# Four adaLN layers in one program: the ternary network starts between the turns of its LayerNorm, chunk sums move to the end of a chunk, and local attention loads early

## What is computed

```python
h = layernorm(x) * (1 + ca) + sa;  x = x + ga * attn(h)
h = layernorm(x) * (1 + cb) + sb;  x = x + gb * ffn(h)
```

```python
h = silu((x @ w1.T) * s1) * ((x @ w2.T) * s2)
h = gelu((h @ h1.T) * sh1);  h = gelu((h @ h2.T) * sh2);  return (h @ w3.T) * s3
```

## Time and profile before

| | |
|---|---|
| time, median of 3 runs | 3133.0 us (3131.6 to 3141.1) |
| profiled execution | 3132.21 us, span 3130.4 us |
| busy, share of the span | TensorE 91%, VectorE 73%, ScalarE 64%, GpSimd 40% |
| chain that ended last | TensorE 66%, VectorE 11%, issue 10%, ScalarE 7% |
| mean granted TensorE clock | 0.928 of full speed |

### The profile page before, as it was taken

One profiled execution on the slowest core, in us unless ns is written; L12 is line 12 of the kernel. 1 busy time (PEld: TensorE's weight loads), 2 busy tenths in 40 slices (PEclk: granted clock), 3 DMA queues, 4 the chain that ended last, 5 costly groups with the idle time before them and its releaser, 6 DMA issues.

```text
span 3130.4 us, 88186 instructions
## 1 busy us (share of the span) xinstructions
PE 2859.3 (91%) x36340; PEld 1713.5 (55%) x36340; DVE 2283.3 (73%) x3908; ACT 2010.7 (64%) x5733; POOL 1239.3 (40%) x959
## 2 busy tenths in 40 slices
PE   5689898878898999998699999999999999999997
PEld 3454577523344233333366666666666666666664
DVE  4740486289604777775688888888888888888885
ACT  5542565274313466666488888878888778887784
POOL 0110012000001111111477766766766776677662
PEclk7589955889999899999799999999999999999999
DMA  2000100000001100000332223323332333322221
GB/s 108 3 1 0 38 4 3 1 0 1 0 0 36 46 24 23 21 23 9 134 72 69 73 65 103 76 65 99 69 81 63 96 81 70 93 65 68 68 62 48
DMA packets 48240, 153.41 MB, mean 49 GB/s; under 512 B 11552, under 2 KB 13856, under 8 KB 45952
## 3 DMA queue, kind: packets, MB, share of 16 engines
q1 hardware_dynamic: 47872, 148.17, 18.1%
HBM read 43.60 MB, written 5.44 MB: 16 GB/s over the span
## 4 chain that ended last, share of the span: by engine, by line
PE 66%; DVE 11%; issue 10%; ACT 7%; POOL 2%; DVEq 1%; POOLq 1%; DMA 1%; ACTq 0%; SPq 0%
PE ps L1675 14%; PE ps L798 7%; PE ps L1693 5%; PE ps L1728 5%; DVE arena L1174 4%; PE ps L1737 4%; PE ps L1750 4%; PE ps L1269 4%; PE ps L1297 3%; PE ps L1710 3%; PE ps L1284 3%; PE ps L1719 3%; PE ps L1756 2%; DVE arena L2143 1%; PE ps L1702 1%
## 5 line engine op out<-in xcount | busy, mean ns | idle before, releaser
L1675 PE MATMUL ps<-arena 128*128 128x512 f32 x1152 | 562.0, 610 | 17.9 <-ACTq L1962 16.3
L2027 ACT ACTIVATE arena<-ps,arena 128x64 f32<-128x64 f32 x1536 | 460.1, 320 | 86.5 <-DVE arena L2223 81.4
L2300 POOL TENSOR_TENSOR arena<-arena 128x1024 f32<-128x1024 f32 x190 | 447.6, 2361 | 98.5 <-DVE arena L2112 98.5
L2306 POOL TENSOR_TENSOR arena<-arena 128x2048 f32<-128x2048 f32 x95 | 344.4, 3625 | 225.0 <-ACT arena L1969 219.8
L1435 DVE TENSOR_REDUCE arena<-ps 128x1 f32<-128x512 f32 x512 | 329.3, 686 | 78.1 <-PE ps L1269 73.1
L1396 ACT ACTIVATE arena<-ps 128x1024 f32<-128x1024 f32 x256 | 262.5, 1025 | 179.1 <-PE ps L1284 178.6
L2027 ACT ACTIVATION_READ_ACCUMULATOR arena<-ps,arena 128x1 f32 x1536 | 324.1, 211 | 0.0
L1675 PEld LDWEIGHTS ps<-arena 128*128 128x128 f32 x1152 | 196.9, 190 | 182.6 <-issue 158.0
L2107 DVE TENSOR_TENSOR arena<-ps,arena 128x1024 f32<-128x1024 f32 x192 | 234.1, 1219 | 47.8 <-PE ps L1675 33.3
L194 POOL TENSOR_SCALAR rstd<-mv 128x4 f32<-128x4 f32 x32 | 7.3, 227 | 645.6 <-DVE mv L180 644.4
L2112 DVE TENSOR_TENSOR arena<-ps,arena 128x512 f32<-128x512 f32 x384 | 245.3, 680 | 0.0
(11 more groups left out here) (291 smaller groups left out, 5560.5 us busy)
## 6 DMA issues: line engine op xcount, KB each, us to landing
arena<-pack_l SPq DMA_DIRECT2D x144, 256.0 KB
arena<-grow SPq DMA_DIRECT2D x144, 256.0 KB
arena<-in_deep SPq DMA_DIRECT2D x6, 2649.5 KB, 10.8
arena<-pack_l SPq DMA_DIRECT2D x96, 128.0 KB
arena<-grow SPq DMA_DIRECT2D x84, 128.0 KB
arena<-in_rotary SPq DMA_DIRECT2D x6, 1024.0 KB, 7.4
pack_tern<-in_tern SPq DMA_DIRECT2D x2, 2888.0 KB, 10.4
arena<-scr_q SPq DMA_DIRECT2D x96, 48.0 KB
```

Source lines behind the costliest of these rows:

```text
L1675: last = T.matmul(m.ps[0:rows.stop - rows.start, at + half, :], f.xs[t % 2][:, rows], w.wqkv[:, j * INNER + half * BLK:j * INNER + (half + ...
L2027: last = A(f.prob[:, p, :], m.ps[:, 4 + j % 2, i * SPAN:(i + 1) * SPAN], ACT.Exp, bias=f.nmax[t % 2][:, p:p + 1], accum_out=f.rsum[t % 2][ ...
L2300: G.tensor_tensor(f.rot[t % 2][:, here], f.rot[t % 2][:, here], f.sin[:, here], ALU.add)
L2306: G.tensor_tensor(r, r, spread(f.ss[t % 2], DH), ALU.mult).then_inc(s["rotated"], 1)
```

## The change

Five edits go together.

1. **Chunk sums at the end.** In `gla_vector` the two calls `summed(n - 1)` and `normed(n - 2)` move from ahead of the level work to behind it. In `gla_scalar`, for layer 0, `squares(n - 1)` moves ahead of the second part of the exponentials.
2. **Ternary networks between the turns.** In layers 0 and 2 the meeting ahead of the feed-forward part goes (`MEETINGS` lists those that stay). `tern_tensor` now issues the turns itself: 0 and 1, pair 0, turn 2, pair 1, turn 3, pair 2. Each of the first four pairs waits for as many modulations as its blocks and banks need, by a new semaphore `modulated`. The sixth LayerNorm turns into banks 4 to 7.
3. **First batch in the last pair.** In `mha_tensor` the turn and the output products of batch 0 (`flat(0)`, `projected(0)`) are issued within the last pair; VectorE copies the turned tiles instead of ScalarE, and adds blocks 0 and 1 before it normalises batch 1. The output products go to other banks (`MHA_OUT`).
4. **Attention's first loads.** VectorE clears only the first operand set, GpSimd the other three, and SyncE waits for GpSimd (`vcopied`) ahead of stacks 1 and 2. ScalarE issues the deep stage's first weights and first rotary table before its first exponential, once regrouping has landed; SyncE no longer does so after the meeting.
5. **Two semaphores less.** The loads of the constants and of the modulation weights share one semaphore, and the first Silu waits for both.

The eighth LayerNorm has its own place for the normalised tiles (`m.xn` is now a list), so that it doesn't touch the early table.

```diff
 def mod_scalar(nc, act, m, s):
-    act.wait_ge(m.loaded["const"], 16)
+    act.wait_ge(m.loaded["const"], 32)
...
-LN_BANKS = (0, 4, 0, 4, 0, 0, 0, 4)
+LN_BANKS = (0, 4, 0, 4, 0, 4, 0, 4)
...
         for pair in range(pairs):
             picks(n, pair)
+        if g.layer == 0 and n:
+            squares(n - 1)
         if quarter >= 1:
             decays(quarter + 1, ahead[2:])
         if g.layer == 1:
             squares(n)
-        elif n:
-            squares(n - 1)
...
-        if n:
-            summed(n - 1)
-        if n >= 2:
-            normed(n - 2)
         if quarter + 1 < TILES // CHUNKS:
...
             differences(quarter + 2, LEVEL_OPS[:4])
+        if n:
+            summed(n - 1)
+        if n >= 2:
+            normed(n - 2)
...
+    k = 2 * f.layer + 1
+    ln_tensor(nc, pe, m, ln, k, (0, 1))
     pe.wait_ge(m.loaded["tern"], f.loaded)
...
             if n >= 4:
                 pe.wait_ge(s["glu"], f.done["glu"] + n - 3)
+            if n in (1, 2):
+                ln_tensor(nc, pe, m, ln, k, (n + 1,))
+            if n == 1 and f.layer == 2:
+                pe.wait_ge(ln["stats"], NBLK * (k + 1))
+            if n < 4:
+                pe.wait_ge(ln["modulated"], NBLK * k + (1, 1, 2, 4)[n])
...
+            if last and par == RING - 1:
+                if kt == 1:
+                    flat(0)
+                if kt == 4:
+                    projected(0)
...
+    act.wait_ge(s["grouped"], 2 * 8 * 16)
+    act.dma_start(deep.wbuf[0], m.d["deep"][0]).then_inc(deep_s["weights"][0], 16)
+    act.dma_start(deep.tab_flat[0], m.d["rotary"]).then_inc(deep_s["rotary"], 16)
     pair_steps(act, step)
     collect(ROUNDS - 1, RING - 1)
     place(ROUNDS - 1, RING - 1)
-    for b in range(BATCH):
-        act.wait_ge(s["flat"], b + 1)
-        A(f.oT[b].rearrange("p (a b) -> p a b", a=2), m.ps[:, 2 * b:2 * b + 2, :], ACT.Copy).then_inc(s["oT"], 1)
+    act.wait_ge(s["flat"], BATCH)
+    A(f.oT[1].rearrange("p (a b) -> p a b", a=2), m.ps[:, 2:4, :], ACT.Copy).then_inc(s["oT"], 1)
...
-    for par in range(RING):
-
-        V.memset(f.kst[par][64:96, :], 0.0)
-        V.memset(f.qst[par][64:P, :], 0.0)
-        V.memset(f.kst[par][96:P, :], 1.0)
+    V.memset(f.kst[0][64:96, :], 0.0)
+    V.memset(f.qst[0][64:P, :], 0.0)
+    V.memset(f.kst[0][96:P, :], 1.0)
...
+    normed(0)
+    dve.wait_ge(s["flat"], 1)
+    V.tensor_copy(f.oT[0].rearrange("p (a b) -> p a b", a=2), m.ps[:, 0:2, :]).then_inc(s["oT"], 1)
+    added(0)
+    added(1)
+    normed(1)
+    added(2)
+    added(3)
...
+    for par in range(1, RING):
+        nc.gpsimd.memset(f.kst[par][64:96, :], 0.0)
...
     for n in range(LEAD + 1):
+        if n:
+            sp.wait_ge(s["vcopied"], n + 1)
         stacks(0, n)
...
-    rotary(0)
-    weights(0)
     rotary(1)
     weights(1)
...
-                ln_tensor(nc, pe, m, ln, 2 * l + 1)
-                finish_stage(pe, m, 2 + 2 * l)
+                if l not in (0, 2):
+                    ln_tensor(nc, pe, m, ln, 2 * l + 1)
+                if l not in (0, 2):
+                    finish_stage(pe, m, MEETINGS.index(2 * l + 1))
```

More of the change, by code:

```diff
@@ L1462, in mha_vector, with normed @@
     pair_steps(dve, step)
-    for b in range(BATCH):
+    def normed(b):
         dve.wait_ge(s["o_read"], HEADS * (b + 1))
@@ L1487, in mha_gpsimd @@
         nc.gpsimd.memset(f.vst[par][:, :, KD:KD + 1], 1.0)
+    pool.drain()
+    for par in range(1, RING):
+        nc.gpsimd.memset(f.kst[par][64:96, :], 0.0)
+    pool.drain()
+    for par in range(1, RING):
+        nc.gpsimd.memset(f.qst[par][64:P, :], 0.0)
+    pool.drain()
+    for par in range(1, RING):
+        nc.gpsimd.memset(f.kst[par][96:P, :], 1.0)
     pool.drain()
```

110 lines of the change are left out of this document (65 added, 45 removed).

## The result

The changed kernel took 3103.5 us (median of 4 runs, 3102.4 to 3106.0), the kernel before 3134.9 on the same chip (4 runs, 3131.6 to 3141.1): ratio 0.990, interval 0.9885 to 0.9916. The forecast was 3108 in a range of 3101 to 3118, "faster by over 0.3%" with a chance of 0.93. Sign and range held; the gain was some 30 us where 24.2 were forecast. A second set on another occasion gave 3103.1 against 3132.6 (ratio 0.9907, 0.9891 to 0.9924). Two single executions further down, one of 4036.8 us with the early loads alone and one of 3358.2 us with the products in the idle time, had a mean granted clock of 0.65 and 0.81 where all others had 0.925 to 0.933; the medians leave them out.

The account below looks back on a forecast made before the run. TensorE was taken to bound local attention and the deep stage, so only seams and layer 0's gated attention could pay. Terms -12.5 - 3.6 - 3.6 - 5.2 + 0.3 + 0.4 = -24.2 us, from 3132.2 to 3108 us; range 3101 to 3118.

Parts of the forecast that it names:

- What bounds the kernel: Local attention and the deep stage are TensorE's own; the change pays only at the seams and in layer 0's gated attention.
- Chunk sums: Layer 0, chunks 1 to 10: level work covers VectorE's ten waits for ScalarE's square, 13.5 us; -12.5 us, ends -6 and -13.5.
- A chunk cannot be shorter than: Layer 0, worked out on chunk 5: picks and TensorE's update product keep a chunk at 5.30 us or more.
- rival A: Layer 0 chunks: VectorE waits for the update product instead; -6 instead of -12.5 us, 3114.5 us; chance 0.10.
- Ternary networks: Layers 0 and 2: pairs start between LayerNorm turns; -1.9 and -1.7, together -3.6 us, ends -1.6 and -5.4.
- The wait of about 1 us for VectorE: Ternary networks: sign that TensorE's fifth pair follows a wait for VectorE of about 1 us.
- Local attention's start: Before the first scores: three quarters of VectorE's clearing goes to GpSimd; -3.6 us, ends -2 and -4.
- Deep weights and table early: Deep stage's start: ScalarE's early loads let the first rotation start at 1501.4 instead of 1506.62; -5.2 us, ends -3 and -6.6.
- Rival B: Local attention: early 3.7 MB collide with the row-maxima round trip, shifting it by up to 8 us; 3116 us; chance 0.08.
- First batch in the last pair: End of local attention: what moves out is paid for by what moves in; +0.3 us, ends -0.5 and +2.
- Start of the program: Program start: the first Silu also waits for the modulation weights; +0.4 us, ends 0 and +0.6.
- Rivals C and D: C: deep stage loses clock, 3142 us or more, chance 0.03; D: other waits at seams, only sums pay, 3120, 0.07.

Follow-up runs that it names:

- the experiment with the early table: Changed kernel plus one unread Silu behind the second modulation in layers 0 and 2, so the Silu table loads earlier: 3102.4 us (3101.4 to 3104.1).

## Why the prediction was right, and where it was off

- **What bounds the kernel**: right. Local attention's pairs moved by under 0.05 us from their first scores to the last pair. The deep stage kept its length but for one drop of the clock.
- **Chunk sums**, -12.5: measured -12.1 in the ten chunks. What did not come back is 1.4 us, not the 1 us forecast, and it has another make-up: 0.8 is chunk 8, which waits 0.60 us for the update product that it copies, a wait that the prediction does not have; the others give back 0.06 to 0.2 us each, and chunk 7 gains 0.1 more than its wait. "A chunk cannot be shorter than" 5.30 us is right for the chunk that it was worked out for and wrong for all: two of the ten took 4.64 and 5.23 us. In chunk 5 the new bound was 0.14 us away, so rival A, which had 0.10, was near in the rows and true only in chunk 8. The last five chunks, which keep their order, took 1.1 us more, with the granted clock at 0.50 instead of 0.67, and the norm's end 0.9 less.
- **Ternary networks**, -1.9 and -1.7: measured -3.4 and -3.2 (alone -2.6 and -3.3). The failed step is "Pair 4 waits for" the second gated product. The code says pair n waits for pair n - 4, so pair 4 waits for the first; the second ended 0.7 us later, and I had merged the two because the row of before shows them as one (x2). The estimate of TensorE's own row, ready 11.4 us after the last statistics, was right to 0.5 us (10.9), and the experiment with the early table shows that this row stands 0.35 us behind. The early Silu was 0.5 us and came as 1.0. Last, the forecast took the start of pair 4's weight load, 198.76, for the start of the pair; the matmuls started 0.43 us later, at 199.19, and in the changed kernel both start together. These three make up the 1.5 us by which the term of layer 0 was too small. The wait of about 1 us for VectorE, named as a sign, is 1.05 us ahead of the weight load and 0.22 ahead of the matmul.
- **Local attention's start**, -3.6: the edit is worth 4.0, in the changed kernel and alone. "ScalarE's conversions between take a little back" was the wrong part of the step. They took nothing: the second subtraction came 4.8 us earlier after the meeting where 3.9 were expected, 0.8 of it the clock's, and the last conversion also 4.8 us earlier. The remaining 0.9 of the 4.9 us are that clock and 0.1 of transfers.
- **Deep weights and table early**, -5.2: measured -5.2, and alone -5.2. "What is late next is VectorE's own clearing and casts" was right, and taking it away gave the next 5.5 us. Rival B's collision happened and cost nothing, as weighed. The "seven to eight us" of slack agree with the 7 us worked out above; a delayed write leaves room within it, a delayed write and read together do not.
- **First batch in the last pair**, +0.3: measured +0.3, undone 0.0.
- **Start of the program**, +0.4: measured +0.2, and +0.5 with the ternary edit alone; but three kernels without this edit start +0.06, +0.44 and +0.46 us from the same trace of before, so the term is not shown.
- **Sum**: 24.2 forecast, 29.8 in the traces. Of the 5.6 missing, 3.0 are the two ternary seams, 1.3 local attention's start (0.4 the term, 0.8 the clock), 1.4 the one drop of the clock late in the deep stage of before; the rest cancels. The forecast left the clock at zero everywhere, and 2.2 of the 5.6 us (0.8 and 1.4 above) are the clock's: that part of the distance is neither a merit nor a fault of the forecast. The range held narrowly: the traces lie 29.8 us apart, and with every term at its low end the prediction had 30. Two terms fell outside their own ends, the ternary networks with 6.6 us against at most 5.4 and local attention's start with 4.9 against at most 4. What kept the total in was that the other terms did not reach their low ends.
- **Rivals C and D**: neither happened. The deep stage's granted clock is 0.99 in both traces, and every seam that was forecast to pay did.

One thing stays open. The ternary edit alone gained 11.4 us in the medians where its two seams hold 5.9; most of the rest of the trace's gain lies in layer 1, where the granted clock rises and falls at other points. The second half of layer 1 is shorter than in the trace of before by 2.4 to 4.4 us in the nine traces of kernels without the two meetings, and by 0.2, 2.5, 2.7 and 2.8 us in the four that keep them. So up to 2.8 us of it come without a removed meeting; whether the removed meetings add the rest no run tells.

## What to carry to other kernels

When a wait is hidden behind independent work, compute the next bound from the same rows down to the tenth; here it said 5.30 against 5.35, and the edit paid 12.1 of 13.5 us. Do it for each kind of repetition: the chunk that copies its state instead of updating it had a wait of its own, and most of the missing 1.4 us. When a buffer is reused n steps later, write down which producer that names before reading a merged row: "x2" hid the difference between the first and the second product, 0.7 of the 1.5 us by which a seam was misjudged. And products taken out of a saturated stage pay only if they go where the engine idles: moved into the last pair they were worth nothing, moved into the 3.1 us gap behind it 2.3 us in one trace and 2.8 in another, 0.9 of it by a clock that fell later.

## What the runs showed of the hardware

- TensorE's granted clock placed its changes differently from execution to execution, and stretches that no edit touches moved by up to 4.4 us. The same instructions of layer 1, of before and of the changed kernel (the first 47 us of its gated attention):

```profile
353.00:400.00 47.00, 40.34 (x532) 24.76 (x532) 26.38 (x58) 37.21 (x72) 0.00 (x0) 0.86 0.17 64
```

```profile
338.00:385.00 47.00, 40.56 (x460) 24.70 (x461) 25.02 (x54) 37.65 (x72) 0.00 (x0) 0.83 0.16 64
```

  The changed kernel starts these 47 us at -15.0 and has 0.83 instead of 0.86, and stands at -13.7 behind them. At the other end, the drop in the deep stage of before:

```profile
3060.00:3080.00 20.00, 18.09 (x320) 13.77 (x321) 10.58 (x20) 14.60 (x51) 6.82 (x5) 0.91 0.23 54
```

```profile
3030.50:3050.50 20.00, 18.09 (x355) 13.15 (x353) 11.69 (x21) 15.89 (x58) 7.86 (x5) 1.00 0.23 54
```

  0.91 against 1.00 in a stretch in which TensorE is busy 18.09 of 20 us: 1.4 us.
- A 6 KB write that met loads of 3.7 MB took 6.1 us instead of 1.3, and 5.96 with 3.0 MB more queued behind.
